# The routing of a per-sample expert convolution: DMA order, column groups of one product, order of the filter bands

## The chip, the cores and the metric

One core of a Trainium2 chip runs the whole program in one launch. The metric is device time in microseconds (us), the median of several runs. "TensorE" or PE is the matrix engine, DVE the vector engine, ACT the scalar engine, POOL is GpSimd, SP the engine whose queue issues the DMAs here (SPq).

## The reference, cut to what matters

The input is 4 images of 64 channels and 128x128 pixels. Four stages follow each other, each `x = x + stage(group_norm(x))`. The change touches the second, a grouped 3x3 convolution whose filters are mixed per image out of four experts:

```
p  = x.reshape(b, c, 16, h//16, 16, w//16).mean(axis=(3, 5))          # pooled to 16x16
r  = relu(einsum('bcij,oc->boij', p, conv_w) + conv_b)                # 16 channels
r  = relu(r.reshape(b, -1) @ fc_w.T + fc_b)                           # 4096 -> 256
rw = sigmoid(r.reshape(b, 4, c))                                      # a gate for each expert and channel
cw = einsum('beo,eoikl->boikl', rw, w_experts)                        # the filters of this image
out = conv3x3(x, cw, feature_group_count=16)
```

The group norm of each stage needs sums over the whole image, so a stage can't start before the one before it has ended. The routing (all lines up to `cw`) needs the whole image too, and the convolution needs `cw`.

## The kernel before, in words

Two images lie side by side on the 128 partitions (64 channels each), and a loop goes twice over such a pair. `X` holds the two images in SBUF. Everything in this text happens between the end of the first stage and the end of the second, once in each pass of that loop.

**Windows.** The convolution works on windows: nine windows of 16 rows, with 8 channels of one image times 16 rows on the partitions. To get there, SP sends `X` to DRAM window by window (L502, `spill`, 1 MB each) and reads each window back in the other layout (`spread`, L489 to L494, into `WN`, in pieces of 512 B). `spread(w)` waits until window `w` has landed in DRAM. The last of them sets `l1_in` to its full count, for which ACT waits (L1879) before it normalizes the first of 16 units (`normed_window`, L1883).

**Order on SP's queue** (L496 to L506). Before the last window's spill SP waits for the last sum of squares of ACT (L499) and sends the four pieces of the routing weights (`FCT`, L501, 1 MB each; `fc_in[0]` counts the first two, `fc_in[1]` the others). Then come the spill of window 8, `spread(7)`, `spread(8)`, and last the table `RT` (L506, 832 KB), which holds the bias `FCB`, the expert filters `EXPW` and the selection matrix `PICK`.

**Product with the weights.** PE (L2172 to L2178) forms the 4096-to-256 product of both images as 32 matmuls, 16 channels `o` times two halves `h` of the 256 pooled pixels. Each has 2 columns of weights (the two images) and streams 256 columns of `FCT`; all accumulate in `PSUM[0:2, 1]`. At `o = 0` PE waits for `fc_in[0]`, at `o = 8` for `fc_in[1]`. A float32 matmul appears in the trace as two passes, so 32 matmuls are 64 records.

**Gates.** DVE waits for the product and for `RT` (L1463, L1464), adds the bias (L1465), takes the maximum with 0 (L1467), ACT takes the exponential (L1878), DVE adds 1 and takes the reciprocal (L1469, L1471). Four small matmuls of PE (L2182) spread the 256 gates over the partitions, into bank 2 of PSUM, in two column groups (output partitions 0 to 63 and 64 to 127).

**Filters and bands.** DVE multiplies `EXPW` with the gates for both images `b` (L1476), and then for each `b` sums over the four experts (L1482, L1485) and writes the values `VAL` (L1488). `toeplitz` (L736 to L752) turns the values of one unit into a banded matrix `WIDE`, by three multiplications (L745) and two additions (L752). DVE makes the bands of units 0 and 1 (`V_UNITS = 2`) after the values of `b = 0` and before those of `b = 1`; POOL makes those of units 2 to 15, after it has waited for all values (`l1_val`, L1689). Units 0 to 7 need the values of `b = 0` only, units 8 to 15 those of `b = 1`.

**Convolution.** PE (L2196 to L2208) takes the 16 units in order, each 9 matmuls of 384 columns (18 records), after `l1_xn` (the unit is normalized) and `l1_tv` or `l1_tp` (its bands are made). ACT evacuates each unit (L1893), DVE adds the residual and takes statistics (L1503 to L1514), SP sends it back to DRAM (L510). For unit 1 ACT waits for all values first (L1889), since its buffer shares memory with the products of `b = 1`.

Of the kernel before, what the change touches and what calls it, by code (L numbers as in the profile page):

```python
# [8 lines left out]
ALU = mybir.AluOpType  # L9
# [4 lines left out]
BATCH, C, H, W = 4, 64, 128, 128  # L14
P = 2 * C
# [13 lines left out]
EXPERTS, RED, FC = 4, 16, 256  # L29
# [51 lines left out]
UNITS = P // WCH  # L81
# [33 lines left out]
def program(nc, x, vec, mat, dts, rows, fc, sel, far_sel, cst, out):  # L115
    ctx = ExitStack()
    with ctx:
# [37 lines left out]
        rt_spill = nc.dram_tensor("rt_spill", (P, NRT), F32).ap()  # L155
# [33 lines left out]
        PSUM = ctx.enter_context(nc.psum_tensor("PSUM", [P, 8, 512], F32))  # L189
# [64 lines left out]
        FS = POOLED  # L254
# [4 lines left out]
        FCT = r.take(RED, 2, FC)  # L259
        RB = r.take(2, 2 * RED)  # L260
        r.at = NREG - TOK - NRT
        RT = r.take(NRT)
        EXPW = RT[:, 0:EXPT]
        FCB = RT[:, EXPT:EXPT + FC]
        PICK = RT[:, EXPT + FC:NRT].rearrange("p (s m) -> p s m", s=2)
# [61 lines left out]
        def steps(*ns):  # L327
# [16 lines left out]
        rt_in, rt_saved = sem("rt_in"), sem("rt_saved")  # L344
        l1_in, l1_xn, l1_sq, l1_pool, l1_mom, l1_bc_pe = steps(
            "l1_in", "l1_xn", "l1_sq", "l1_pool", "l1_mom", "l1_bc_pe")
        l1_val, l1_tv, l1_tp, l1_mm, from_psum, l1_res, l1_st = steps(
            "l1_val", "l1_tv", "l1_tp", "l1_mm", "from_psum", "l1_res", "l1_st")
# [4 lines left out]
        rt_pe, rt_dve, rt_act = sem("rt_pe"), sem("rt_dve"), sem("rt_act")  # L353
# [18 lines left out]
        def settle(eng):  # L372

            eng.sem_inc(settled, 1)
# [89 lines left out]
        def _(sp):  # L464
# [22 lines left out]
            with sp.Fori(0, PAIRS) as pair:  # L487
# [8 lines left out]
                for w in range(WINDOWS):  # L496
                    sp.wait_ge(o_x, pair * NS + (window_strip(w) + 1 + CREDIT))
                    if w == WINDOWS - 1:
                        sp.wait_ge(l1_sq, (pair + 1) * (2 * NS) + CREDIT)  # L499
                        for j in range(4):  # L500
                            sp.dma_start(FCT[:, 4 * j:4 * j + 4], fc[:, 4 * j:4 * j + 4]).then_inc(fc_in[j // 2], 16)  # L501
                    sp.dma_start(spill[w], X[:, STEP * w:STEP * w + WROW, :].rearrange("p r x -> p (r x)")).then_inc(moved[w % 2], 16)  # L502
                    if w >= 1:
                        spread(w - 1)
                spread(WINDOWS - 1)
                sp.dma_start(RT, rt_spill).then_inc(rt_in, 16)  # L506

                for u in range(UNITS):
                    sp.wait_ge(l1_res, pair * UNITS + (u + 1))
# [244 lines left out]
        V_UNITS = 2  # L754
# [348 lines left out]
        def _(dve):  # L1103
# [37 lines left out]
            for s in range(2):  # L1141
                p, q = s * C, s * C + C
# [15 lines left out]
            for s in range(2):  # L1158
                p, q = s * C, s * C + C
                ins = dve.tensor_tensor(W3[p:q, 1, 1, :], W3[p:q, 1, 1, :], NOT3[p:q, p:q], ALU.add)  # L1160
# [7 lines left out]
            for m, half in ((1, 0.5), (2, -0.5)):  # L1168
                ins = dve.scalar_tensor_tensor(out=WCOL[:, :, m, :], in0=W3[:, :, 1, :], scalar=half, in1=W3H,
                                               op0=ALU.mult, op1=ALU.add)  # L1170
# [91 lines left out]
            with dve.Fori(0, PAIRS) as pair:  # L1262
# [193 lines left out]
                q0 = pair * 16  # L1456
# [7 lines left out]
                dve.wait_ge(rt_in, pair * 16 + 16)  # L1464
                dve.tensor_tensor(FS[0:2, :], PSUM[0:2, 1, 0:FC], FCB[0:2, :], ALU.add).then_inc(rt_dve, 1)  # L1465
                dve.wait_ge(rt_dve, q0 + 3)
                dve.tensor_scalar(FS[0:2, :], FS[0:2, :], 0.0, None, ALU.max).then_inc(rt_dve, 1)  # L1467
                dve.wait_ge(rt_act, pair + 1)
                dve.tensor_scalar(FS[0:2, :], FS[0:2, :], 1.0, None, ALU.add).then_inc(rt_dve, 1)  # L1469
                dve.wait_ge(rt_dve, q0 + 5)  # L1470
                dve.reciprocal(FS[0:2, :], FS[0:2, :]).then_inc(rt_dve, 11)  # L1471
                dve.wait_ge(rt_pe, pair * 3 + 3)
                v0 = pair * 16
                n = EXPT // 4
                for b in range(2):
                    dve.tensor_tensor(EPROD[:, b].rearrange("p (a t o) -> p a t o", t=9, o=4),  # L1476
                                      EXPW.rearrange("p (a t o) -> p a t o", t=9, o=4),
                                      PSUM[:, 2, b * P:(b + 1) * P].rearrange("p (a o) -> p a o", o=4).unsqueeze(
                                          2).broadcast_to([P, 32, 9, 4]), ALU.mult).then_inc(l1_val, 1)
                for b in range(2):  # L1480
                    dve.wait_ge(l1_val, v0 + 2 + b if b == 0 else v0 + 6)
                    dve.tensor_tensor(EPROD[:, b, 0:2 * n], EPROD[:, b, 0:2 * n], EPROD[:, b, 2 * n:4 * n],  # L1482
                                      ALU.add).then_inc(l1_val, 1)
                    dve.wait_ge(l1_val, v0 + 4 + 3 * b)
                    dve.tensor_tensor(EPROD[:, b, 0:n], EPROD[:, b, 0:n], EPROD[:, b, n:2 * n], ALU.add).then_inc(l1_val, 1)  # L1485
                    dve.wait_ge(l1_val, v0 + 5 + 3 * b)
                    for h in range(2):
                        ins = dve.tensor_scalar(  # L1488
                            VAL[:, b].rearrange("p k (t c) -> p (k t) c", c=WCH)[:, :, 4 * h:4 * h + 4],
                            EPROD[:, b, 0:n].rearrange("p (a o) -> p a o", o=4), HALF2[:, h:h + 1], None, ALU.mult)  # L1490
                    ins.then_inc(l1_val, 1)
                    if b == 0:
                        dve.wait_ge(l1_val, v0 + 6)
                        for u in range(V_UNITS):
                            toeplitz(dve, l1_tv, pair * 16 + 5 * u, u == 0, u)
                dve.wait_ge(l1_tv, pair * 16 + 5 * V_UNITS)
                dve.sem_inc(l1_tv, 16 - 5 * V_UNITS)
                dve.sem_inc(l1_val, 7)

                for u in range(UNITS):  # L1500
# [151 lines left out]
        def _(pool):  # L1652
            credit(pool, cv_pool, df_w9, df_r1, df_lo, df_add, sc_u)
            pool.memset(PAD[:, :, :], 0.0).then_inc(border, 1)
            with pool.Fori(0, PAIRS) as pair:
# [30 lines left out]

                in_turn(pool, NS // 2, 0, 0, step)

                pool.wait_ge(l1_val, (pair + 1) * 16)  # L1689
                settle(pool)  # L1690
                for u in range(V_UNITS, UNITS):
                    if u >= RING:
                        pool.wait_ge(l1_mm, pair * UNITS + (u - RING + 1))
                        settle(pool)
                    toeplitz(pool, l1_tp, pair * (5 * (UNITS - V_UNITS)) + 5 * (u - V_UNITS), u == V_UNITS, u)
# [50 lines left out]
        def _(act):  # L1746
# [31 lines left out]
            with act.Fori(0, PAIRS) as pair:  # L1778
# [94 lines left out]

                group_norm(pair * 4 + 1)
                act.wait_ge(l1_mom, pair * 16 + 6)
                act.wait_ge(rt_dve, pair * 16 + 4)
                settle(act)
                act.activation(FS[0:2, :], FS[0:2, :], ACT.Exp, scale=-1.0).then_inc(rt_act, 1)  # L1878
                act.wait_ge(l1_in, (pair + 1) * (WINDOWS * 16))  # L1879
# [112 lines left out]
        def _(pe):  # L1992
# [40 lines left out]
            with pe.Fori(0, PAIRS) as pair:  # L2033
# [138 lines left out]
                for o in range(RED):  # L2172
                    if o % 8 == 0:
                        pe.wait_ge(fc_in[o // 8], pair * 32 + 32)
                    for h in range(2):
                        ins = pe.matmul(PSUM[0:2, 1, 0:FC], RB[:, h, :].rearrange("p (s o) -> p o s", s=2)[:, o, :],
                                        FCT[:, o, h, :], start=(o + h == 0), stop=(o == RED - 1 and h == 1))
                ins.then_inc(rt_pe, 1)  # L2178
                pe.wait_ge(rt_dve, pair * 16 + 6)
                for s in range(2):  # L2180
                    for h in range(2):
                        ins = pe.matmul(PSUM[h * C:(h + 1) * C, 2, s * P:(s + 1) * P], PICK[0:2, s, 0:C],  # L2182
                                        FS[0:2, :].rearrange("p (a h o) -> p a h o", h=2, o=4)[:, :, h, :],
                                        start=True, stop=True)
                ins.then_inc(rt_pe, 1)
# [189 lines left out]
```

## Time and profile before

| | |
|---|---|
| time, median of 3 runs | 2608.61 us (2603.66 to 2608.94) |
| span of the profiled execution, first to last instruction | 2604.5 us |
| time of the profiled execution beyond its span | not given on its own; the median of the runs is 4.1 us above that span |
| PE / DVE / ACT / POOL busy | 83% / 74% / 56% / 55% |
| DMA, mean over the span | 60 GB/s |

The span runs from the first to the last instruction. Busy shares are averages over stages of different kinds. Around the change (340 to 481 us for the first pair, 1617 to 1758 us for the second) each stage waits for the one before it, and what counts is the chain of waits in that stretch.

### The profile page before, as it was taken

What the parts mean: (1) busy time and instruction counts of PE and PEld (TensorE: products, weight loads), DVE (VectorE), ACT (ScalarE), POOL (GpSimd) and SP (SyncE); (2) the same over time, 40 slices, a digit from 0 to 9 for tenths busy, and PEclk for the clock granted to TensorE, in tenths of its full rate; (3) what the DMA queues carried; (4) which work ended last, traced back from release to release, by engine and by line L of the source; (5) the groups of instructions that cost most, each with busy time, mean ns of one, the idle gap of its engine ahead of it and who ended that gap; (6) DMA issues with size and microseconds to landing.
All of it is one profiled execution on the core that took longest, in us unless ns stands there. A gap on an engine that the chain in (4) does not pass through costs nothing.

```text
span 2604.5 us, 29243 instructions
## 1 busy us (share of the span) xinstructions
PE 2174.7 (83%) x7607; PEld 1139.6 (44%) x7607; DVE 1932.7 (74%) x3308; ACT 1452.4 (56%) x2268; POOL 1425.8 (55%) x1287
## 2 busy tenths in 40 slices
PE   3898859897968989986988977798789589999788
PEld 2397525443543333332335964353344333333243
DVE  6656746598957999994755668466899399999754
ACT  1743534385865676663346436236678467667532
POOL 2231009378947888872322400475799388888532
PEclk9988879898979999998988989899999799999999
DMA  4000363400000010013820007333000001011145
GB/s 177 1 1 1 136 233 100 175 1 0 1 2 1 17 33 17 17 33 114 242 53 0 1 1 275 130 101 138 1 1 1 3 9 25 17 24 26 51 122 121
DMA packets 131751, 155.97 MB, mean 60 GB/s; under 512 B 4951, under 2 KB 107743, under 8 KB 128247
## 3 DMA queue, kind: packets, MB, share of 16 engines
q1 hardware_dynamic: 131575, 154.00, 19.3%
q8 instruction: 65, 1.06, 0.2%
q14 instruction: 111, 0.91, 0.1%
HBM read 81.69 MB, written 72.29 MB: 59 GB/s over the span
## 4 chain that ended last, share of the span: by engine, by line
PE 39%; DVE 23%; issue 14%; POOL 13%; ACT 5%; DMA 3%; SPq 1%; DVEq 1%; POOLq 0%; ACTq 0%
PE PSUM L2207 7%; PE PSUM L704 7%; POOL BIG L903 6%; PE PSUM L2028 4%; DVE BIG L819 3%; POOL BIG L1733 3%; DVE BIG L843 3%; POOL BIG L1728 3%; PE PSUM L2071 3%; PE PSUM L2085 2%; PE PSUM L2227 2%; DVE PSUM L1086 2%; DVE BIG L850 2%; DVE PSUM L826 2%; DVE BIG L864 2%
## 5 line engine op out<-in xcount | busy, mean ns | idle before, releaser
L903 POOL TENSOR_TENSOR BIG<-BIG 128x512 f32<-128x512 f32 x320 | 406.9, 1272 | 106.1 <-DVE BIG L864 84.3
L819 DVE TENSOR_TENSOR BIG<-PSUM,BIG 128x512 f32<-128x512 f32 x576 | 378.7, 686 | 71.1 <-PE PSUM L1013 28.2
L1086 DVE SCALAR_TENSOR_TENSOR PSUM<-BIG,VECS,PSUM 128x1024 f32<-128x1024 f32 x224 | 288.3, 1287 | 40.3 <-PE PSUM L2028 35.0
L745 POOL TENSOR_TENSOR BIG<-TOEP,BIG 128x384 f32<-128x384 f32 x84 | 97.2, 1183 | 340.5 <-DVE BIG L1488 340.5
L1013 PE MATMUL PSUM<-BIG,SELB 120*128 120x512 bf16 x576 | 211.9, 388 | 81.5 <-DVE BIG L819 73.7
L2028 PE MATMUL PSUM<-BIG,WDW 128*128 128x512 f32 x512 | 233.5, 600 | 11.3 <-ACT BIG L1932 11.3
L2207 PE MATMUL PSUM<-BIG 128*128 128x381 f32 (+1 forms) x576 | 190.4, 494 | 15.2 <-DVE BIG L752 15.2
L1019 PE MATMUL PSUM<-BIG,CSTS 128*128 128x512 f32 x384 | 200.6, 604 | 0.0
L1013 PEld LDWEIGHTS PSUM<-BIG,SELB 120*128 120x128 bf16 x576 | 55.9, 97 | 276.1 <-DVE BIG L819 182.7
L2028 PEld LDWEIGHTS PSUM<-BIG,WDW 128*128 128x128 f32 x512 | 96.7, 192 | 139.2 <-issue 115.5
L1733 POOL TENSOR_TENSOR BIG<-BIG 128x1024 f32<-128x1024 f32 x64 | 150.9, 2357 | 11.7 <-POOL BIG L1728 11.7
L2207 PEld LDWEIGHTS PSUM<-BIG 128*128 128x128 f32 x576 | 111.8, 194 | 93.3 <-issue 20.6
L704 PE MATMUL PSUM<-BIG,WL 128*128 128x512 f32 x256 | 119.5, 610 | 15.5 <-POOL BIG L689 12.3
L955 ACT ACTIVATE BIG<-BIG 128x320 bf16<-128x320 f32 x64 | 30.1, 470 | 168.0 <-POOL BIG L928 168.0
L688 POOL TENSOR_TENSOR BIG<-BIG 128x576 f32<-128x576 f32 x32 | 39.1, 1222 | 153.2 <-issue 96.1
L1706 POOL TENSOR_TENSOR BIG<-BIG 128x1024 f32<-128x1024 f32 x32 | 75.6, 2362 | 77.6 <-ACT BIG L1920 77.6
L1728 POOL TENSOR_SCALAR BIG<-BIG,VECS,CSTS 128x1024 f32<-128x1024 f32 x96 | 114.2, 1196 | 6.8 <-POOL BIG L1733 6.8
L704 PE MATMUL PSUM<-BIG,WMID 128*128 128x512 f32 x256 | 115.5, 594 | 0.3 <-DVE BIG L679 0.2
L1893 ACT ACTIVATE BIG<-PSUM,SMG 128x1152 f32<-128x1152 f32 x32 | 39.0, 1220 | 136.0 <-PE PSUM L2207 113.2
L1019 PEld LDWEIGHTS PSUM<-BIG,CSTS 128*128 128x128 f32 x384 | 75.1, 196 | 74.6 <-issue 69.8
L2260 PE MATMUL PSUM<-BIG,CSTS 128*128 128x512 f32 x128 | 69.8, 672 | 45.3 <-DVE BIG L1086 45.2
L919 POOL TENSOR_TENSOR BIG<-BIG 128x96 f32<-128x96 f32 x192 | 69.1, 389 | 64.8 <-ACT BIG L964 64.8
(362 smaller groups left out, 5387.5 us busy)
## 6 DMA issues: line engine op xcount, KB each, us to landing
spill<-X SPq DMA_DIRECT2D x18, 1024.0 KB, 6.1
back_spill<-BIG SPq DMA_DIRECT2D x32, 576.0 KB, 3.4
X<-x SPq DMA_DIRECT2D x32, 512.0 KB, 7.9
rows_spill<-X SPq DMA_DIRECT2D x64, 256.0 KB, 4.1
out<-BIG SPq DMA_DIRECT2D x64, 256.0 KB, 3.6
BIG<-rows_spill SPq DMA_DIRECT2D x28, 512.0 KB, 5.1
X<-back_spill SPq DMA_DIRECT2D x14, 896.0 KB, 11.6
BIG<-fc SPq DMA_DIRECT2D x8, 1024.0 KB, 9.6
```

Source lines behind the costliest of these rows:

```text
L704: ins = pe.matmul(PSUM[:, 4 * k + m, :].rearrange("p (r j) -> p r j", r=8), w, VC[:, k, m, b:b + 8, :], start=(b == 0), stop=(b == 1))
L745: eng.tensor_tensor(to.rearrange("p (x c r) -> p x c r", x=3, r=WROW), TOEP[:, y].unsqueeze(1).unsqueeze(1).broadcast_to([P, 3, WCH, WROW] ...
L819: dve.tensor_tensor(img(o), img(PSUM[:, (k + q) % 2, :]), pch(c, XBASE, dy, dx), ALU.mult).then_inc(df_p, 1)
L843: dve.tensor_tensor_scan(HH[:, k, :], DA, PSUM[:, BB, :], SM[:, 12:13] if first else HH[:, 1 - k, CH - 1:CH], ALU.mult, ALU.add).then_inc( ...
L903: pool.tensor_tensor(XS[:, k, :], XS[:, k, :], product_buffer(q), ALU.add).then_inc(df_add, 1)
L1013: pe.matmul(PSUM[:, (k + q) % 2, :], SELB[:, q, :], WTB[0:WROWS, k, h * CH:(h + 1) * CH], start=True, stop=True).then_inc(df_w, 1)
L1019: pe.matmul(PSUM[:, ACC, :], ident, PRD[:, m % 2, :], start=(m == 0), stop=(m == PE_SUMS - 1)).then_inc(df_acc, 1)
L1086: return dve.scalar_tensor_tensor(out=rows8(to), in0=strip(c, base, dy, dx), scalar=vc(weights, j), in1=rows8(acc), op0=ALU.mult, op1=ALU.add)
L1728: pool.tensor_scalar(rows8(d_tap if n else d_side[:, c % 2, :]), strip(c, XBASE, dy, dx), vc("dw_w", j), cs("zero")[:, 0:1], ALU.mult, ALU ...
L1733: pool.tensor_tensor(d_side[:, c % 2, :], d_side[:, c % 2, :], d_tap, ALU.add).then_inc(d1_part, 1)
L2028: ins = pe.matmul(img(acc[:, h * CH:(h + 1) * CH]), w[:, j - stored, :], strip(c, base, dy, dx)[:, h * ROWS:(h + 1) * ROWS, :], start=(j = ...
L2207: ins = pe.matmul(to, WIDE[:, u % RING, x, :], v, start=(x == 1), stop=(x == 2))
```

## The change

In the sync block the load of `RT` moves from behind the last `spread` to behind the four loads of `FCT`, which is ahead of the last spill. The product with the weights goes to two column groups: the half `h = 0` accumulates in `PSUM[0:2, 1]`, the half `h = 1` in `PSUM[64:66, 1]`, and DVE adds the second by one more instruction. The gates are spread into bank 6 instead of bank 2. DVE makes products, values and the bands of units 0 and 1 for `b = 0` first, releases POOL by `l1_tv`, and then does all of `b = 1`; POOL waits for the values of `b = 1` only ahead of unit 8. The counts of the semaphores follow.

```diff
                             sp.dma_start(FCT[:, 4 * j:4 * j + 4], fc[:, 4 * j:4 * j + 4]).then_inc(fc_in[j // 2], 16)
+                        sp.dma_start(RT, rt_spill).then_inc(rt_in, 16)
                     sp.dma_start(spill[w], ...).then_inc(moved[w % 2], 16)
                     if w >= 1:
                         spread(w - 1)
                 spread(WINDOWS - 1)
-                sp.dma_start(RT, rt_spill).then_inc(rt_in, 16)
...
                 dve.tensor_tensor(FS[0:2, :], PSUM[0:2, 1, 0:FC], FCB[0:2, :], ALU.add).then_inc(rt_dve, 1)
                 dve.wait_ge(rt_dve, q0 + 3)
+                dve.tensor_tensor(FS[0:2, :], PSUM[C:C + 2, 1, 0:FC], FS[0:2, :], ALU.add).then_inc(rt_dve, 1)
+                dve.wait_ge(rt_dve, q0 + 4)
                 dve.tensor_scalar(FS[0:2, :], FS[0:2, :], 0.0, None, ALU.max).then_inc(rt_dve, 1)
...
                 for b in range(2):
                     dve.tensor_tensor(EPROD[:, b]..., EXPW...,
-                                      PSUM[:, 2, b * P:(b + 1) * P]..., ALU.mult).then_inc(l1_val, 1)
+                                      PSUM[:, 6, b * P:(b + 1) * P]..., ALU.mult).then_inc(l1_val, 1)
-                for b in range(2):
-                    dve.wait_ge(l1_val, v0 + 2 + b if b == 0 else v0 + 6)
+                    dve.wait_ge(l1_val, v0 + 2 + 4 * b)
                     dve.tensor_tensor(EPROD[:, b, 0:2 * n], ...).then_inc(l1_val, 1)
...
                     if b == 0:
-                        dve.wait_ge(l1_val, v0 + 6)
+                        dve.wait_ge(l1_val, v0 + 5)
                         for u in range(V_UNITS):
                             toeplitz(dve, l1_tv, pair * 16 + 5 * u, u == 0, u)
-                dve.wait_ge(l1_tv, pair * 16 + 5 * V_UNITS)
-                dve.sem_inc(l1_tv, 16 - 5 * V_UNITS)
+                        dve.wait_ge(l1_tv, pair * 16 + 5 * V_UNITS)
+                        dve.sem_inc(l1_tv, 16 - 5 * V_UNITS)
                 dve.sem_inc(l1_val, 7)
...
-                pool.wait_ge(l1_val, (pair + 1) * 16)
+                pool.wait_ge(l1_tv, (pair + 1) * 16)
                 settle(pool)
                 for u in range(V_UNITS, UNITS):
+                    if u == UNITS // 2:
+                        pool.wait_ge(l1_val, (pair + 1) * 16)
+                        settle(pool)
...
                     for h in range(2):
-                        ins = pe.matmul(PSUM[0:2, 1, 0:FC], RB[:, h, :]..., FCT[:, o, h, :],
-                                        start=(o + h == 0), stop=(o == RED - 1 and h == 1))
+                        ins = pe.matmul(PSUM[h * C:h * C + 2, 1, 0:FC], RB[:, h, :]..., FCT[:, o, h, :],
+                                        start=(o == 0), stop=(o == RED - 1))
...
-                        ins = pe.matmul(PSUM[h * C:(h + 1) * C, 2, s * P:(s + 1) * P], PICK[0:2, s, 0:C],
+                        ins = pe.matmul(PSUM[h * C:(h + 1) * C, 6, s * P:(s + 1) * P], PICK[0:2, s, 0:C],
```

## Rows read from the trace of the kernel before

**Rows 1.** The page: span, busy time and share of each engine.
```profile
span 2604.5 us, 29243 instructions
PE 2174.7 (83%) x7607; PEld 1139.6 (44%) x7607; DVE 1932.7 (74%) x3308; ACT 1452.4 (56%) x2268; POOL 1425.8 (55%) x1287
```

**Rows 2.** Chain of waits, 330 to 400 us: start, length, what (engine or DMA, line).
```profile
345.23 15.96 DMA spill<-X
362.05 7.73 DMA BIG<-rt_spill
369.87 0.42 DVE BIG L1465
374.12 2.62 DVE BIG L1476 x2
381.68 18.59 PE PSUM L2207 x48
```

**Rows 3.** Timeline, 325 to 400 us: start, length, engine, line, idle before.
```profile
352.44 16.18 PE L2176 MATMUL PSUM<-BIG 128*2 128x256 f32 x64 [4.83 <-DMA BIG<-fc]
352.82 0.13 PEld L2176 LDWEIGHTS PSUM<-BIG 128*2 128x2 f32 x1 [0.30 <-issue]
356.66 0.13 PEld L2176 LDWEIGHTS PSUM<-BIG 128*2 128x2 f32 x1 [0.30 <-issue]
370.32 0.28 DVE L1467 TENSOR_SCALAR BIG<-BIG 2x256 f32<-2x256 f32 x1
371.12 6.29 ACT L1883 ACTIVATE BIG<-BIG,SMG 128x1152 f32<-128x1152 f32 x5
373.42 0.65 PE L2182 MATMUL PSUM<-BIG 2*64 2x128 f32 x8 [4.81 <-DVE BIG L1471]
383.08 1.26 DVE L752 TENSOR_TENSOR BIG<-BIG 128x384 f32<-128x384 f32 x2
384.26 0.75 DVE L1482 TENSOR_TENSOR BIG<-BIG 128x576 f32<-128x576 f32 x1
386.37 2.42 POOL L745 TENSOR_TENSOR BIG<-TOEP,BIG 128x384 f32<-128x384 f32 x3 [171.15 <-DVE BIG L1488]
```

**Rows 4.** Busy time by stretch, with the granted clock (PEclk), DMA share, GB/s.
```profile
352.40:356.80 4.40, 4.36 (x11) 1.38 (x12) 0.00 (x0) 0.00 (x0) 0.00 (x0) 0.50 1.02 354
356.80:361.00 4.20, 4.20 (x21) 1.62 (x19) 0.00 (x0) 0.00 (x0) 0.00 (x0) 0.99 1.00 381
381.60:386.00 4.40, 4.32 (x7) 2.51 (x8) 4.04 (x9) 0.00 (x0) 0.00 (x0) 0.50 0.00 0
```

**Rows 5.** Timeline, 364 to 369 us, PE alone.
```profile
363.70 4.91 PE L2176 MATMUL PSUM<-BIG 128*2 128x256 f32 x22
```

**Rows 6.** DMAs issued at 344.76, 345.23, 361.33 and 362.05: size, us to landing.
```profile
BIG<-fc SPq DMA_DIRECT2D x1, 1024.0 KB, 13.9
spill<-X SPq DMA_DIRECT2D x1, 1024.0 KB, 16.0
BIG<-spill SPq DMA_DIRECT2D x1, 0.5 KB, 6.4
BIG<-rt_spill SPq DMA_DIRECT2D x1, 832.0 KB, 7.7
```

**Rows 7.** Timeline, 1610 to 1690 us, the second pair.
```profile
1629.65 15.87 PE L2176 MATMUL PSUM<-BIG 128*2 128x256 f32 x64 [4.54 <-DMA BIG<-fc]
1647.48 0.41 DVE L1465 TENSOR_TENSOR BIG<-PSUM,BIG 2x256 f32<-2x256 f32 x1 [21.89 <-DMA BIG<-rt_spill]
1659.75 30.69 PE L2207 MATMUL PSUM<-BIG 128*128 128x384 f32 x88 [7.60 <-DVE BIG L752]
```

**Rows 8.** Line L2207, the convolution: what PE waited for, over both pairs.
```profile
  DVE BIG L752: 15.2, 2
```

**Rows 9.** Timeline, 466 to 500 us.
```profile
465.56 11.71 PE L2207 MATMUL PSUM<-BIG 128*128 128x384 f32 x36
466.27 0.99 POOL L752 TENSOR_TENSOR BIG<-BIG 128x384 f32<-128x384 f32 x1 [0.18 <-POOL BIG L752]
```

More of the change, by code:

```diff
@@ L1469, in _ @@
                 dve.tensor_scalar(FS[0:2, :], FS[0:2, :], 1.0, None, ALU.add).then_inc(rt_dve, 1)
-                dve.wait_ge(rt_dve, q0 + 5)
-                dve.reciprocal(FS[0:2, :], FS[0:2, :]).then_inc(rt_dve, 11)
+                dve.wait_ge(rt_dve, q0 + 6)
+                dve.reciprocal(FS[0:2, :], FS[0:2, :]).then_inc(rt_dve, 10)
                 dve.wait_ge(rt_pe, pair * 3 + 3)
@@ L1477, in _ @@
                                       EXPW.rearrange("p (a t o) -> p a t o", t=9, o=4),
-                                      PSUM[:, 2, b * P:(b + 1) * P].rearrange("p (a o) -> p a o", o=4).unsqueeze(
+                                      PSUM[:, 6, b * P:(b + 1) * P].rearrange("p (a o) -> p a o", o=4).unsqueeze(
                                           2).broadcast_to([P, 32, 9, 4]), ALU.mult).then_inc(l1_val, 1)
-                for b in range(2):
-                    dve.wait_ge(l1_val, v0 + 2 + b if b == 0 else v0 + 6)
+                    dve.wait_ge(l1_val, v0 + 2 + 4 * b)
                     dve.tensor_tensor(EPROD[:, b, 0:2 * n], EPROD[:, b, 0:2 * n], EPROD[:, b, 2 * n:4 * n],
                                       ALU.add).then_inc(l1_val, 1)
-                    dve.wait_ge(l1_val, v0 + 4 + 3 * b)
+                    dve.wait_ge(l1_val, v0 + 3 + 4 * b)
                     dve.tensor_tensor(EPROD[:, b, 0:n], EPROD[:, b, 0:n], EPROD[:, b, n:2 * n], ALU.add).then_inc(l1_val, 1)
-                    dve.wait_ge(l1_val, v0 + 5 + 3 * b)
+                    dve.wait_ge(l1_val, v0 + 4 + 4 * b)
                     for h in range(2):
@@ L1875, in _ @@
                 act.wait_ge(l1_mom, pair * 16 + 6)
-                act.wait_ge(rt_dve, pair * 16 + 4)
+                act.wait_ge(rt_dve, pair * 16 + 5)
                 settle(act)
@@ L2175, in _ @@
                     for h in range(2):
-                        ins = pe.matmul(PSUM[0:2, 1, 0:FC], RB[:, h, :].rearrange("p (s o) -> p o s", s=2)[:, o, :],
-                                        FCT[:, o, h, :], start=(o + h == 0), stop=(o == RED - 1 and h == 1))
+                        ins = pe.matmul(PSUM[h * C:h * C + 2, 1, 0:FC], RB[:, h, :].rearrange("p (s o) -> p o s", s=2)[:, o, :],
+                                        FCT[:, o, h, :], start=(o == 0), stop=(o == RED - 1))
                 ins.then_inc(rt_pe, 1)
-                pe.wait_ge(rt_dve, pair * 16 + 6)
+                pe.wait_ge(rt_dve, pair * 16 + 16)
                 for s in range(2):
                     for h in range(2):
-                        ins = pe.matmul(PSUM[h * C:(h + 1) * C, 2, s * P:(s + 1) * P], PICK[0:2, s, 0:C],
+                        ins = pe.matmul(PSUM[h * C:(h + 1) * C, 6, s * P:(s + 1) * P], PICK[0:2, s, 0:C],
                                         FS[0:2, :].rearrange("p (a h o) -> p a h o", h=2, o=4)[:, :, h, :],
```

## The prediction

> **What bounds the kernel now.** The page gives PE 83% and DVE 74% of the span [rows 1], an average over stages with different limits, so the place of the change has to be read by itself. I read four views, in this order. The chain of waits between the first stage's end and the first matmul of the convolution is the main one [rows 2]: it holds almost no PE work. From 345.23 to 361.2 it is the last spill on its way to DRAM, then the table `RT` behind the last spread, which lands at 362.05 + 7.7 = 369.8 [rows 2, 6], and from 369.87 to 381.68 a string of short DVE, ACT and PE steps up to the first convolution matmul. The reader is to see that the table ends the wait of L1465, with the product close behind it: PE's 64 passes run from 352.44 to 352.44 + 16.18 = 368.6 [rows 3], 1.2 us before the table. Second, the timeline of the convolution: once started PE waits for nobody; the only wait of L2207 on an engine is the first one of each pair, 15.2 us in 2 times, for the bands of unit 0 [rows 8]. So whatever brings the first matmul of L2207 forward brings the end of the stage forward by as much, and every later stage, since each needs sums over the whole image. Third, the landing times [rows 6], since a DMA moved ahead of others delays them. Fourth, the stretches with the granted clock [rows 4].
>
> **The change part by part**, worked out for the first pair; the second is the same shape, with its own start times.
>
> *The table sent ahead.* It stands on SP's queue behind the four weight loads and ahead of spill 8, spread 7 and spread 8. The last weight load lands at 344.76 + 13.9 = 358.7, spill 8 at 345.23 + 16.0 = 361.2, 2.5 us later for 1 MB [rows 6]. At that rate 832 KB take 2.0 us, so the table lands near 360.7, and spill 8, both spreads and `l1_in` come 2.0 us later. `l1_in` lies at 361.33 + 6.4 = 367.7 now [rows 6], at 369.8 then. What does that hold up? ACT's normalization of unit 0, at 6.29 / 5 = 1.26 us a unit (I take 1.4) [rows 3]: unit 0 is ready at about 369.8 + 0.2 + 1.4 = 371.4. That is a floor for PE, used below. The bounds: nothing at all if the rings have room, and 7.7 us, the whole time of the table in its own row. I take 2.0, the rate of the neighbouring transfer. The issue itself is 2 us or less on SP, and SP then only waits for a spill that is on the rings until 361: hidden.
>
> *Two column groups.* Now each pass starts when the one before it has streamed. At the low clock (0.50, 1.2 GHz) ten loads stand from 352.82 to 356.66, 3.84 / 9 = 0.427 us apart; at the full clock (2.4 GHz) 22 passes take 4.91 us, of which the last is 0.38, so (4.91 - 0.38) / 21 = 0.216 us apart [rows 3 to 5]. Do passes to two column groups run at once? No row shows this product so, but one shows such a pair of groups: L2182, 8 passes of 128 columns in 0.65 us [rows 3]. One pass of 256 columns takes 0.216, so one of 128 takes 0.108; eight in turn would take 0.86 us and the end of the last one on top. They took 0.65, which fits four slots of 0.108 and an end of 0.2. So two passes share a slot. I apply that: 32 slots instead of 64. The low clock lasts until 356.8 [rows 4], that is 10 slots (20 passes); the 12 left of the first half of the weights take 6 x 0.216 = 1.3, to 358.1. There PE now meets a wait that it did not have before: the second half lands at 358.7. Then 16 slots x 0.216 = 3.5 and an end of 0.16: the product is complete at 362.4, 6.2 us earlier, and the table is there (360.7). Bounds: from this to no overlap at all, 368.6.
>
> A rule that speaks against this part: the Trainium skill, "TensorE: Matmul & The Clock Gate", section "Packing small matmuls — row/col tiling", says that a weight load overlaps running matmuls only where the row groups differ, and here both groups use all rows. The trace disagrees for loads under matmuls of the same rows: L2176's loads stand inside a PE stretch without a gap [rows 3]. The same section measured 2.38x for three column groups; by that share two groups would give 1.59x and a slot of 0.27 us, which makes the product end 1.2 us later than my sum.
>
> *The added addition.* One DVE instruction of 2x256 reading PSUM; the one like it is the first L1465, from 369.87 to the start of L1467 at 370.32 [rows 2, 3]: +0.45 us on the path. Bounds: 0.28, the cheaper form of the same size, and 0.45.
>
> *`b = 0` first.* Of the two L1476 (2.62 us together [rows 2]) one leaves the path: -1.31, and a wait for its own result comes in, for which the neighbours show about 0.1: -1.2. The steps of `b = 1` (1.3 for its product, 0.75 for L1482 [rows 3], and the rest until POOL's start at 386.4) now lie behind the second band. Nothing needs them before ACT's second evacuation and DVE's first residual, more than 9 us after PE's start: hidden. If that cover failed it would cost up to 1.3 + 386.4 - 384.3 = 3.4 us.
>
> *POOL released earlier.* POOL starts now at 386.37 [rows 3] and finishes unit 15 at 466.27 + 0.99 = 467.3 [rows 9]. PE needs it 4 us after that (its work ends at 465.56 + 11.71 = 477.3 [rows 9], and a unit takes 5.8, half of that row). So POOL isn't the bound before. After the change it starts when DVE's second band is done, 383.08 + 1.26 - 381.68 = 2.7 us after PE's start instead of 4.7 [rows 2, 3]: its margin grows by 2 us. POOL and DVE are then busy together for 3 us, where they were not; even at 1.1 us more for the first unit the margin stays. Worth: nothing. Bank 6 instead of 2 costs nothing: it only lets PE write unit 0 while DVE still reads the gates.
>
> *Sum.* From the start of L1465 to the first L2207 it is 381.68 - 369.87 = 11.81 now, and 11.81 + 0.45 - 1.2 = 11.06 then. L1465 starts at 362.45, so L2207 at 373.5, above the floor of 371.4. Gain 8.2 us. Second pair [rows 7]: product from 1629.65; its clock rises after about 3.9 us, so 9 slots low and 7 high give 1635.0; the second half of the weights, lying as in the first pair, lands near 1636.1, product ends 1639.7; the chain is 1659.75 - 1647.48 + 0.45 - 1.2 = 11.5; L2207 at 1651.3, gain 8.5. Together 16.7 us. In either pair PE begins the convolution at the low clock, as it does now (0.50 from 381.6 to 386 [rows 4]), since it idles 6 us ahead of it; where the rise falls may shift it by 1 us each way. Against the profiled execution: span 2604.5 - 16.7 = 2587.8; what lies around that span is not given, and the median of the runs is 4.1 above it, so I put the time at 2608.6 - 16.7 = 2591.9.
>
> **The rivals.**
>
> *No overlap.* The passes to two groups run one after the other. For it: no row has two groups with 128 rows and a long stream. Against it: L2182's 0.65 us. The product then ends at 368.6 and 1645.5, the table no longer ends the wait, and L1465 starts 1.2 and 1.9 us earlier; with 0.75 of the shorter chain each the gain is 2.0 + 2.7 = 4.7: 2603.9 us.
>
> *The windows become the bound.* The table pushes `l1_in` so far that unit 0's normalization is later than its bands. My margin is 373.5 - 371.4 = 2.1 us; it decides when the table costs the rings more than 4.1 us. For it: its own 7.7 us from issue to landing [rows 6], and the rings are full from 352 to 361 (share 1.0) [rows 4]. Against it: it is smaller than a transfer that took 2.5. At 7.7, unit 0 is ready at 377.1, the gain is 4.6 a pair: 2599.4 us.
>
> *Slower: loads exposed.* If, with column groups, a load had to wait until the pass of the other group is through, each of the 64 passes would take its whole 0.38 plus its load, 0.46 at the full clock and more at the low one: about 32 us for the product, an end near 385 and a loss of 15 - 0.8 = 14 us a pair: 2637 us. It turns the sign when the product takes over 352.44 to 370.6, 18.2 us, or 0.28 us a pass; L2182 had a pass every 0.08 to 0.11 at half the columns.
>
> That the change doesn't do what it says is the first rival for the product; for the DMA it can't be, the order on the queue is the program's.
>
> **How the numbers follow.** Forecast 0.75, no overlap 0.12, windows as the bound 0.09, slower 0.03, 0.01 for others. The forecast's own range is 2588 to 2596 (partial overlap adds 2.4 us in two pairs, the clock's rise 2, and the runs of before are 5 us apart). The range reaches to the windows' case: 2586 to 2600, and leaves out the 0.15 of no overlap and slower. 0.2% (5.2 us) is about what a measurement of this kernel can tell from no change. Faster by more than that: forecast and windows' case, 0.84. Within it: no overlap, 0.12. Slower: 0.04.
>
> **What the changed kernel's profile would show.** L2176: 64 passes in some 10 us, with a short wait for the second half of the weights; starts in pairs. L1465 ended by PE, not by the table, at about 362.4. `l1_in`'s last spread landing 2 us later than now. L1883 starting before L2207 and not ending its wait. L2207's first matmul at about 373.5 and 16 units without a gap behind it; POOL starting about 376. If L2176 takes 16 us again, the overlap was wrong; if L2207's first wait ends on ACT L1883, the cost of the table on the rings was; if L2207 waits for POOL or ACT in the middle, the cover of `b = 1` was.

## The result, and the profile after

The changed kernel takes 2593.27 us (median of 6 runs, 2591.36 to 2598.74) against 2608.36 us (6 runs): 0.9938 of the time before, 95% interval 0.9922 to 0.9954, some 16 us faster. The span of its profiled execution is 2589.1 us, 15.4 below the 2604.5 of [rows 1].

The chain of waits of the first pair is the place to look. Columns: start, length, what.

```profile
344.38 8.53 DMA BIG<-fc
352.95 8.85 PE PSUM L2180 x64
361.83 0.42 DVE BIG L1465
362.27 0.43 DVE BIG L1467
366.54 1.36 DVE BIG L1478
372.96 27.27 PE PSUM L2211 x78
```

Two links are gone: the last spill's 15.96 us and the table's 7.73 us of [rows 2] stand in the chain no more. In their place are the weights' transfer and the product itself (line 2180 now, 2176 before). The timeline has the rest; its columns are start, length, engine, line, and the idle time before with what ended it:

```profile
352.95 8.82 PE L2180 MATMUL PSUM<-BIG 128*2 128x256 f32 x64 [5.62 <-DMA BIG<-fc]
353.34 0.13 PEld L2180 LDWEIGHTS PSUM<-BIG 128*2 128x2 f32 x2 [0.29 <-issue]
353.76 0.13 PEld L2180 LDWEIGHTS PSUM<-BIG 128*2 128x2 f32 x2 [0.29 <-issue]
361.83 0.41 DVE L1465 TENSOR_TENSOR BIG<-PSUM,BIG 2x256 f32<-2x256 f32 x1 [14.00 <-PE PSUM L2180]
370.70 6.30 ACT L1887 ACTIVATE BIG<-BIG,SMG 128x1152 f32<-128x1152 f32 x5 [7.08 <-DMA BIG<-spill]
372.96 22.46 PE L2211 MATMUL PSUM<-BIG 128*128 128x384 f32 x63 [6.47 <-DVE BIG L752]
375.86 2.94 POOL L745 TENSOR_TENSOR BIG<-TOEP,BIG 128x384 f32<-128x384 f32 x3 [159.28 <-DVEq L1498]
```

The same 64 passes take 8.82 us where they took 16.18 [rows 3]; the loads come two at a time, still 0.42 us apart at the low clock. The first addition is released by PE, no longer by the table, and the first convolution matmul comes at 372.96 instead of 381.68 [rows 2]. In the second pair the trace names another releaser:

```profile
1639.31 2.25 PE L2211 MATMUL PSUM<-BIG 128*128 128x384 f32 x3 [6.47 <-ACT BIG L1887]
```

The prediction took a wait that ends on ACT's normalization (L1887 now, L1883 before) as the sign that the table had cost the rings too much. Here it isn't. In the first pair PE starts before ACT is done with its second unit, so it needs the first alone, and that one was ready at 1638.05. The bands of unit 0 (L752) were done at 1639.16, 0.15 us before PE's start, as in the first pair; it is ACT's second unit that happens to end at 1639.29.

All runs below are measured by one number, the **stretch** from the issue of the first load of the group (L501) to the first convolution matmul. It was 381.68 - 341.78 = 39.9 us in the first pair and 1659.75 - 1619.29 = 40.5 in the second. It is now 372.96 - 341.51 = 31.5 and 1639.31 - 1608.61 = 30.7. That is 18.2 us in both pairs, while the span fell by 15.4. The rest was given away where nothing was changed: from the second pair's first convolution matmul to the end of the span it took 2604.5 - 1659.75 = 944.8 us before and 2589.1 - 1639.31 = 949.8 now. The largest piece stands in the second pair's third stage, in the same instructions, before (first fence) and after (second). Columns: stretch, its length, busy us of PE, PEld, DVE, ACT, POOL, then the granted clock:

```profile
2025.00:2035.00 10.00, 5.49 (x26) 3.45 (x24) 1.48 (x2) 7.01 (x9) 0.00 (x0) 0.84 0.00 0
```

```profile
2005.00:2018.00 13.00, 8.49 (x24) 5.19 (x23) 1.48 (x2) 6.47 (x8) 0.00 (x0) 0.50 0.00 0
```

Two dozen matmuls take 8.5 us at 1.2 GHz where they took 5.5 at mostly 2.4 GHz. All three profiled executions of the changed kernel have this piece: the 16 small matmuls in it take 3.43 us in each, against 1.85 before. But it doesn't hang on the change alone, as the kernels b_together, ballast and best2 below have it fast (1.87 to 2.00). The part from the second pair's convolution to the end takes 948.0 to 953.7 us in all runs below. Why the clock falls here in one kernel and there in another stays open; it is why the stretch says more of an edit than one execution's span.

### The profile page after: what moved, and what is told of

Its sections match the earlier page's. It is cut to its first block, busy times and chain, and to the rows that moved or that the text cites. A ratio compares the mean times of both kernels' runs of the same rounds, so it can differ in the third digit from the quotient of the medians.

```text
span 2589.1 us, 29247 instructions
## 1 busy us (share of the span) xinstructions
PE 2157.4 (83%) x7607; PEld 1133.4 (44%) x7607; DVE 1937.9 (75%) x3310; ACT 1453.2 (56%) x2268; POOL 1427.5 (55%) x1287
## 4 chain that ended last, share of the span: by engine, by line
PE 39%; DVE 22%; issue 15%; POOL 13%; ACT 6%; DMA 3%; SPq 1%; DVEq 1%; POOLq 0%; ACTq 0%
PE PSUM L2211 7%; POOL BIG L903 6%; PE PSUM L704 6%; PE PSUM L2032 4%; DVE BIG L819 3%; POOL BIG L1732 3%; POOL BIG L1737 3%; DVE BIG L843 3%; PE PSUM L2075 3%; PE PSUM L2089 2%; PE PSUM L2231 2%; DVE PSUM L1086 2%; DVE BIG L850 2%; DVE PSUM L826 2%; PE PSUM L2047 2%
## 5 line engine op out<-in xcount | busy, mean ns | idle before, releaser
L819 DVE TENSOR_TENSOR BIG<-PSUM,BIG 128x512 f32<-128x512 f32 x576 | 379.0, 687 | 73.3 <-PE PSUM L1013 30.2
L1086 DVE SCALAR_TENSOR_TENSOR PSUM<-BIG,VECS,PSUM 128x1024 f32<-128x1024 f32 x224 | 288.3, 1287 | 38.2 <-PE PSUM L2032 32.5
L2211 PEld LDWEIGHTS PSUM<-BIG 128*128 128x128 f32 x576 | 111.2, 194 | 90.2 <-ACT BIG L1887 13.4
L704 PE MATMUL PSUM<-BIG,WL 128*128 128x512 f32 x256 | 120.1, 613 | 15.4 <-POOL BIG L689 12.3
L955 ACT ACTIVATE BIG<-BIG 128x320 bf16<-128x320 f32 x64 | 30.1, 470 | 167.4 <-POOL BIG L928 167.4
## 6 DMA issues: line engine op xcount, KB each, us to landing
X<-back_spill SPq DMA_DIRECT2D x14, 896.0 KB, 11.6
```

Of the source, the lines that this page charges most:

```text
L704: ins = pe.matmul(PSUM[:, 4 * k + m, :].rearrange("p (r j) -> p r j", r=8), w, VC[:, k, m, b:b + 8, :], start=(b == 0), stop=(b == 1))
L819: dve.tensor_tensor(img(o), img(PSUM[:, (k + q) % 2, :]), pch(c, XBASE, dy, dx), ALU.mult).then_inc(df_p, 1)
L1086: return dve.scalar_tensor_tensor(out=rows8(to), in0=strip(c, base, dy, dx), scalar=vc(weights, j), in1=rows8(acc), op0=ALU.mult, op1=ALU.add)
L2211: ins = pe.matmul(to, WIDE[:, u % RING, x, :], v, start=(x == 1), stop=(x == 2))
```

## The experiments

Four rounds of comparison gave these numbers; "ratio" is to the kernel before in the same rounds. The stretch is from one profiled execution each, first and second pair.

| kernel | stretch, us | median, us | ratio, 95% interval |
|---|---|---|---|
| before | 39.9 / 40.5 | 2608.4 to 2613.2 | 1 |
| after | 31.5 / 30.7 | 2593.3 | 0.9938 (0.9922 to 0.9954) |
| again | 31.0 / 31.5 | 2592.2 | 0.9928 (0.9915 to 0.9942) |
| again_b | 31.0 / 32.0 | 2594.0 | 0.9934 (0.9918 to 0.9950) |
| no_groups | 37.4 / 37.8 | 2602.9 | 0.9968 (0.9956 to 0.9980) |
| table_last | 40.2 / 39.8 | 2612.2 | 1.0003 (0.9993 to 1.0014) |
| b_together | 33.2 / 32.5 | 2594.6 | 0.9923 (0.9908 to 0.9938) |
| best | 31.3 / 31.2 | 2589.0 | 0.9912 (0.9898 to 0.9925) |
| best2 | 30.1 / 30.2 | 2590.5 | 0.9914 (0.9897 to 0.9931) |
| best2_b | 31.3 / 30.2 | 2591.8 | 0.9928 (0.9911 to 0.9944) |
| ballast | 33.5 / 33.1 | 2594.9, one run | |
| four_groups | 31.6 / 31.5 | 2594.2, one run | |
| groups_32 | 31.5 / 31.4 | 2590.8, one run | |
| pool_late | 30.7 / 31.2 | 2589.5, one run | |

Times and stretches agree only to some 3 to 5 us. By its ratio no_groups gains 8.4 us and b_together 20.1; by their stretches, 5.2 and 14.7. The stretch carries the argument below, and the times support it only where the difference is larger than that.

**Theory A**: the two column groups run at once, the table's early load makes that visible, and PE starts the convolution earlier by the sum of both. **Theory B**: one of the two carries the gain alone.

**again** and **again_b**, no edit: the changed kernel beside the others.

> The changed kernel once more, in the same rounds as the next three, as their measure. From the issue of the first weight load to the first convolution matmul it took 31.5 and 30.7 us in the profiled execution after (39.9 and 40.5 before). Expected: the same within 1 us, and 2593 us, 15 less than before. Both theories below expect this.

> The changed kernel once more, as the measure for 'best2_b' in the same rounds: 2592 to 2594 us, stretch from the first weight load to the first convolution matmul 30.7 to 31.5 us.

As expected, except that the second pair of again_b took 32.0 us. Over its six stretches the changed kernel has a mean of 31.3 us with a spread of 1.3. Part of the spread is the clock of the gates' matmuls (L2182 before): they took 0.65 us in four of the six and 1.11 to 1.12 in the second pairs of again and again_b, as in the second pair of the kernel before (1.11).

**no_groups.** One part undone:

```diff
-ins = pe.matmul(PSUM[h * C:h * C + 2, 1, 0:FC], ..., start=(o == 0), stop=(o == RED - 1))
+ins = pe.matmul(PSUM[0:2, 1, 0:FC], ..., start=(o + h == 0), stop=(o == RED - 1 and h == 1))
-dve.tensor_tensor(FS[0:2, :], PSUM[C:C + 2, 1, 0:FC], FS[0:2, :], ALU.add).then_inc(rt_dve, 1)
```

> The changed kernel with the product in one column group again (and without the second addition). Theory A (the two groups run at once, and that is most of the gain): 64 passes take 16 us again, so the product ends near 369 and the first convolution matmul comes at 361.8 -> 369.1, less 0.45 for the addition, 38.3 us after the first weight load; time near 2604, 4 to 5 below before. Theory B (the gain comes from the table being sent ahead, the product's length being hidden by the transfer): the stretch stays near 31 to 33 us and the time near 2594.

Its timeline:

```profile
350.14 16.18 PE L2178 MATMUL PSUM<-BIG 128*2 128x256 f32 x64 [4.58 <-DMA BIG<-fc]
366.36 0.41 DVE L1465 TENSOR_TENSOR BIG<-PSUM,BIG 2x256 f32<-2x256 f32 x1 [20.30 <-PE PSUM L2178]
```

The product is back at 16.18 us (16.04 in the second pair, 15.87 before), and DVE waits for it, while the table had landed 7.6 and 7.1 us before the product's end. 6.3 us of the gain of 8.9 a pair are gone. Theory A holds for the product.

**table_last.** The table's load back behind the last spread:

```diff
-                        sp.dma_start(RT, rt_spill).then_inc(rt_in, 16)
...
                 spread(WINDOWS - 1)
+                sp.dma_start(RT, rt_spill).then_inc(rt_in, 16)
```

> The changed kernel with the table's load back behind the last spread. Theory A: the product still ends near 359 to 362, but the first addition waits for the table, which lands at 369.8, so the stretch is 39.2 us (11.1 us of chain behind it) and the time near 2607: the two parts give their gain only together. Theory B': the column groups carry the gain alone; the stretch is near 32 us. ACT's first normalization should come 2 to 3 us earlier than in the changed kernel (368 instead of 370.7).

```profile
368.48 0.41 DVE L1465 TENSOR_TENSOR BIG<-PSUM,BIG 2x256 f32<-2x256 f32 x1 [22.29 <-DMA BIG<-rt_spill]
370.18 5.04 ACT L1887 ACTIVATE BIG<-BIG,SMG 128x1152 f32<-128x1152 f32 x4
372.48 1.12 PE L2186 MATMUL PSUM<-BIG 2*64 2x128 f32 x8 [11.51 <-DVE BIG L1473]
```

DVE waits for the table again, as in [rows 7], and the whole gain is gone, though the product is fast. Theory B falls on both sides: the groups without the early table give nothing (1.0003), the early table without the groups 0.9968. It is 0.6 to 1.0 us worse than I had expected in the stretch: PE idles 11.5 us ahead of the gates' matmuls and does them at the low clock, 1.12 us for 0.65, and in the first pair the table landed 0.5 us later than before (28.5 us after the first load). The 1.2 us that the order of `b` saves doesn't show either, since the added addition (0.45) and, in the first pair, that low clock (0.47) stand against it. ACT's early normalization did not show; ACT was held behind the exponential, which waits for the same table.

**b_together.** DVE's order of before, and POOL's wait for all values:

```diff
+for b in range(2):
+    dve.tensor_tensor(EPROD[:, b]..., ALU.mult)          # both products first
 for b in range(2):
-    dve.tensor_tensor(EPROD[:, b]..., ALU.mult)
...
-pool.wait_ge(l1_tv, (pair + 1) * 16)
+pool.wait_ge(l1_val, (pair + 1) * 16)
```

> The changed kernel with DVE's order of before: both products (L1476 twice) ahead of the values and bands of the first half, and POOL released only when all values are made. Theory A: only the second product's 1.3 us, less 0.1, comes back on the path: the stretch from the first weight load to the first convolution matmul is 1.2 us longer, 32.2 to 32.7 us, and PE waits for nobody after it, since POOL's unit 2 is ready some 5 us before PE needs it; 2595 us, 2.4 more than the changed kernel, hardly to be told by its time. Rival: POOL's earlier release is worth something of its own; PE would then show waits for POOL in the convolution.

From the first addition to the convolution it is 375.01 - 362.73 = 12.3 and 12.7 us against 11.1 and 11.6 in "again": 1.15 a pair, the term of the sum. The first pair's stretch of 33.2 lies above the range expected, as its last weights landed 13.6 us after their issue and its product ended 20.8 us after the first load, later than in any of the changed kernel's six stretches (19.5 to 20.4). The time can't tell it from the changed kernel. PE waited for POOL nowhere.

**pool_late.** Only POOL's release undone, DVE's order kept:

```diff
 pool.wait_ge(l1_tv, (pair + 1) * 16)
 settle(pool)
+pool.wait_ge(l1_val, (pair + 1) * 16)
+settle(pool)
```

> The changed kernel, but POOL waits for the values of both images again before its first band; DVE's order stays. Theory A: POOL starts 3 us later (about 6 us after PE's first convolution matmul instead of 2.9), DVE's steps of the second image run at 0.75, 0.46 and 0.65 us (they took 0.95, 0.97 and 1.27 beside POOL), PE still waits for nobody after its first matmul, and the stretch and the time are those of the changed kernel. Rival: POOL's early start is part of the gain; then PE waits for bands and the time is some us higher.

```profile
371.23 17.14 PE L2213 MATMUL PSUM<-BIG 128*128 128x384 f32 x46 [6.47 <-DVE BIG L752]
375.44 0.76 DVE L1483 TENSOR_TENSOR BIG<-BIG 128x576 f32<-128x576 f32 x1
376.23 0.46 DVE L1486 TENSOR_TENSOR BIG<-BIG 128x288 f32<-128x288 f32 x1
377.55 2.43 POOL L745 TENSOR_TENSOR BIG<-TOEP,BIG 128x384 f32<-128x384 f32 x3 [162.04 <-DVE BIG L1489]
```

Against the changed kernel, where POOL runs beside these steps:

```profile
377.16 0.95 DVE L1483 TENSOR_TENSOR BIG<-BIG 128x576 f32<-128x576 f32 x1
378.15 0.97 DVE L1486 TENSOR_TENSOR BIG<-BIG 128x288 f32<-128x288 f32 x1
```

The early release is worth nothing: PE's first wait is its only one here too, and the stretch is the same. The release costs DVE 0.2 and 0.5 us on two steps that nobody waits for.

**ballast.** Two more transfers of the table's size ahead of the last spill:

```diff
 sp.dma_start(RT, rt_spill).then_inc(rt_in, 16)
+for j in range(2):
+    sp.dma_start(ballast[j], rt_spill).then_inc(load, 16)    # DRAM to DRAM
```

> The changed kernel with two more transfers as large as the table (832 KB each, DRAM to DRAM, read by nobody) behind the table and ahead of the last spill. Theory A: the product and the gates don't notice (first addition 20.0 to 20.5 us after the first weight load), while the last spread lands 4 to 5 us later: ACT's first normalization starts near 33 us after the first weight load, not 27.6 to 29.2, and ends the wait of the first convolution matmul at 34.5 to 35 us, not 31.0 to 31.5. This is the case 'windows become the bound', forced. Rival: the chain sets the start still, at 31.5, if ballast costs the rings under 2 us in all; or the table itself lands later, if what follows it matters as theory C says.

```profile
359.72 0.41 DVE L1469 TENSOR_TENSOR BIG<-PSUM,BIG 2x256 f32<-2x256 f32 x1 [13.73 <-PE PSUM L2184]
371.79 3.83 ACT L1891 ACTIVATE BIG<-BIG,SMG 128x1152 f32<-128x1152 f32 x3 [10.27 <-DMA BIG<-spill]
373.19 2.28 PE L2215 MATMUL PSUM<-BIG 128*128 128x384 f32 x3 [8.67 <-ACT BIG L1891]
```

The rival "windows become the bound", made real: the first addition keeps its place (20.0 and 19.7 us after the first load), ACT's normalization starts at 32.1 and 31.7 us, and now it ends PE's wait, 1.4 us later. The stretch grew by 2 us, less than the 3.5 expected, as the ballast delayed the windows by about 4 us on a slack of 2. In the six stretches of the changed kernel unit 0 is normalized 0.9 to 2.8 us before PE starts, 1.8 in the mean: so far away is its next bound.

**four_groups** and **groups_32**, on the array:

```diff
+g = 32 * (2 * (o % 2) + h)                                  # four_groups
-ins = pe.matmul(PSUM[h * C:h * C + 2, 1, 0:FC], ...)
+ins = pe.matmul(PSUM[g:g + 2, 1, 0:FC], ...)
+ins = pe.matmul(PSUM[h * 32:h * 32 + 2, 1, 0:FC], ...)      # groups_32
```

> The changed kernel with the product in four column groups (output partitions 0, 32, 64, 96: parity of o times h), and three additions behind it. If four passes run at once: 64 passes in 16 slots, in the first half four starts per slot of 0.427 us; the product waits for the second half of the weights and ends 8 slots (1.7 us) + 0.2 after its landing, near 16.4 + 1.9 = 18.3 us after the first weight load, but the table lands at 20.1 and the two further additions cost 0.9, so the first convolution matmul comes 0.5 to 0.9 us later than in the changed kernel. If only two run at once: two starts per slot, the product ends as in the changed kernel.

```profile
352.04 3.59 PE L2185 MATMUL PSUM<-BIG 128*2 128x256 f32 x32 [4.83 <-DMA BIG<-fc]
357.00 3.26 PE L2185 MATMUL PSUM<-BIG 128*2 128x256 f32 x32 [1.37 <-DMA BIG<-fc]
360.46 0.41 DVE L1465 TENSOR_TENSOR BIG<-PSUM,BIG 2x256 f32<-2x256 f32 x1 [12.75 <-DMA BIG<-rt_spill]
```

```profile
352.00:355.60 3.60, 3.56 (x32) 0.99 (x32) 0.00 (x0) 0.00 (x0) 0.00 (x0) 0.50 1.00 417
357.00:360.30 3.30, 3.26 (x32) 1.00 (x32) 0.00 (x0) 0.00 (x0) 0.00 (x0) 0.58 0.93 384
```

Four passes do run at once: 32 passes in 8 slots of 0.427 and an end. Yet the second half took 3.3 us, not the 1.9 I expected, since the granted clock was low through most of it (0.58). The table (360.4) then held DVE back anyway, and two further additions ate what was left.

> The changed kernel with the second half of the product at output partitions 32 and 33 instead of 64 and 65. Theory A (a group is 32 columns wide for weights of 2 columns, so that neighbours run at once): two starts in every slot as before, product and stretch as in the changed kernel (8.8 to 9.4 us and 30.7 to 31.5). Rival (the array is split in halves of 64): 64 passes in turn, 16 us, stretch 38.

The product took 9.1 and 9.5 us, the stretch 31.5 and 31.4: neighbouring groups of 32 columns do as well as 64 apart, for weights of 2 columns.

**best, best2, best2_b.** A version meant to beat both, and its variant with the filters ahead of the spill:

```diff
+sp.dma_start(RT[0:2, EXPT:NRT], rt_spill[0:2, EXPT:NRT]).then_inc(rt_in, 16)     # 4 KB, first
 for j in range(4):
-    sp.dma_start(FCT...).then_inc(fc_in[j // 2], 16)
+    sp.dma_start(FCT...).then_inc(fc_in[j], 16)
-sp.dma_start(RT, rt_spill).then_inc(rt_in, 16)
+sp.dma_start(EXPW, rt_spill[:, 0:EXPT])...    # best: behind the last spill; best2: here
...
-dve.tensor_scalar(FS, FS, 0.0, None, ALU.max); dve.tensor_scalar(FS, FS, 1.0, None, ALU.add)
+dve.tensor_scalar(FS, FS, 1.0, 1.0, ALU.min, ALU.add)       # after the exponential
```

> Changed kernel with the loads cut to what each step needs: only the two partitions of bias and selection go ahead of the weights, the expert filters go behind the last spill, each quarter of the weights has a semaphore of its own, and the maximum with 0 becomes a minimum with 1 of the exponential, in the instruction that adds 1. Theory A: the product starts 2.5 us earlier and ends 0.2 + 8 slots of 0.216 us behind the last quarter of the weights (about 359.9 instead of 361.8), the chain is 0.45 shorter, and the windows become the bound: the last spread lands near 370, the first convolution matmul comes 1.4 us later, at 371.3 to 371.5 instead of 373.0. The stretch is 30 us (from 31.5), the time 2590 to 2592, not to be told from the changed kernel by its time. A rival: the expert filters behind the spill land too late (after 364.5) and the chain waits for them: stretch 31 or more.

> As 'best', but the expert filters (576 KB) stand behind the weights and ahead of the last spill. In 'best' the last quarter of the weights landed 13.9 us after its issue, with the spill right behind it; in the changed kernel, with the table behind it, 12.6. Theory C (a load lands later when a spill to DRAM stands right behind it on the queue): here it lands after 12.6 again, the product ends near 359.9, the chain gives 371.0 and the windows, 371.4, become the bound: stretch 29.5 to 30.2 us against 31.0 to 31.5. Rival: the landing depends on the rings' total only; it stays at 13.9 and the stretch at 31.

> The kernel 'best2' once more, beside the changed kernel on the same chip. Its stretch was 30.1 and 30.2 us, 2.1 us shorter in both pairs together than the changed kernel's 31.5 + 30.7 (or 31.0 + 31.5). Theory A expects 2 us less in the time, 0.08%: its median 1 to 3 us below that of 'again_b', the intervals overlapping. Rival: the finer waits and split loads cost something elsewhere, and it is not below.

"best" has no shorter stretch than the changed kernel: its last quarter of the weights landed 14.0 and 14.3 us after its issue instead of 12.5 to 13.1, so the earlier start of the product ended in waits of 0.8 and 2.0 us. The chain from the first addition to the convolution shrank by 0.16 us (10.97 for 11.13, first pair), not by the 0.45 expected, and it stayed the bound: PE's wait ends on DVE's bands and not on ACT, in all pairs of best, best2 and best2_b. Its time is lower (2589.0 against 2592.2 in the same rounds, each of its five runs below each of the five of "again"), and I can show no cause for that.

"best2" was to cure the late weights by my theory C and didn't: with a load behind it the last quarter landed after 14.1 and 13.4 us (14.2 and 14.0 in best2_b). In no_groups, where the table stands behind it as in the changed kernel, it landed after 14.3 us in one pair and 12.6 in the other. Theory C falls. Three of the four stretches of best2 are 30.1 to 30.2, 1.1 us below the mean of the changed kernel, one is 31.3. In the only rounds that had both, its median is 2.2 us below that of "again_b", 0.1%, with intervals that overlap. So best2 has the shortest stretches and best the lowest time, and the runs don't prove either better than the changed kernel.

## Why the prediction was right

The forecast was 16.7 us from two earlier starts of the convolution; the six stretches of the changed kernel give 2 x (40.2 - 31.3) = 17.8, the times about 16, 17 and 19 (ratios times 2608 to 2611). That the one forecast time, 2591.9, lies 1.4 us from the measured 2593.3 is in part luck, as the unchanged rest of the kernel moves by more than that from run to run.

The forecast's landing times against those of the six stretches of the changed kernel, in us after the issue of the first weight load, first and second pair of the kernel before:

| | before | forecast | changed kernel (mean) |
|---|---|---|---|
| last of the weights lands | 16.9 / 16.8 | 16.9 | 15.6 to 16.7 (16.0) |
| product complete | 26.8 / 26.2 | 20.6 / 20.4 | 19.5 to 20.4 (20.0) |
| table lands | 28.0 / 28.1 | 18.9 | 18.5 to 20.2 (19.1) |
| last spread lands | 26.0 / 25.9 | 28.0 | 27.5 to 29.1 (28.0) |
| first convolution matmul | 39.9 / 40.5 | 31.7 / 32.0 | 30.7 to 32.0 (31.3) |

- **What bounds it** held: after its first matmul PE waited for nobody in any kernel, and the convolution then took 94.2 to 95.7 us in all of them, so what comes off the stretch comes off the stage, to within 1.5 us.
- **Column groups.** Shown by no_groups and by the double loads. The price of a slot was right; the 0.65 us of L2182 [rows 3] was enough to find it. The estimate from the Trainium skill, "TensorE: Matmul & The Clock Gate", section "Packing small matmuls — row/col tiling", a share of 2.38x for three groups, would have given 1.59x; here 64 passes with the low clock at their start took 8.82 instead of 16.18 us, 1.83x, and four groups ran four to a slot at the low clock. The loads weren't exposed, though both groups use all rows. The product ended some 0.6 us earlier than forecast, because the last weights landed 0.8 us earlier in the mean than in the kernel before, whose landing time I had carried over. That term was off, and it makes the gain 17.8 us instead of 16.7.
- **The table on the rings.** I took 2.0 us for it. In the mean of the six stretches the last spread landed 2.1 us later than before, so the term was right, but the single values lie between 1.5 and 3.1. The profiled execution of the result has the largest: the weights' last quarter landed at 345.32 + 12.6 = 357.9 and the table at 346.05 + 15.6 = 361.65, 0.1 us before the product's end:

```profile
BIG<-rt_spill SPq DMA_DIRECT2D x1, 832.0 KB, 15.6
spill<-X SPq DMA_DIRECT2D x1, 1024.0 KB, 17.7
```

  There the rival "the windows become the bound" was only 0.9 us away (unit 0 ready at 372.05 against 372.96), where I had 2.1 of margin. It happened in none of the six.
- **Added addition**: 362.27 - 361.83 = 0.44 for 0.45. **`b = 0` first**: 1.15 in b_together for 1.2. **Chain**: 11.1 us in four of the six stretches and 11.6 in the two where the gates' matmuls ran at the low clock, for a forecast of 11.06 in the first pair and 11.5 in the second.
- **POOL's release**: worth nothing, shown by pool_late. Its margin was no part of the gain.
- **"No overlap"** was priced at 4.7 us; no_groups, which is that case without the added addition (0.45 a pair, so 5.6 by the same sum), gained 5.2 by its stretches.
- **What I didn't see** is that the two larger parts give their gain only together. I had added up one path, which was right, but with the table last the change is worth nothing, and I had no rival for that.

## What to carry to other kernels

Where several things end close together (here product at 368.6, table at 369.8, windows at 367.7) no single edit shows its worth: price the path after all of them, and ask of each alone what stands right behind it. A matmul with few columns of weights (here 2) and a long stream can be cut over column groups at the cost of one short addition for each further group. What is needed first should be sent first, but only as far as the next bound allows: a table ahead of the windows is paid by the windows.

## What the runs showed of the hardware

Passes to different column groups start in the same slot, with 128 rows, 2 columns of weights and 256 columns streamed: two of them at 1.2 GHz (0.427 us a slot) and at 2.4 GHz (0.216), four of them at 1.2 GHz.

The transfers' rate falls to two thirds for some 2 us near where the loads give way to the spill, and what is in flight then lands late: here the table, in the kernel before and in the first pair of no_groups the last of the weights. The first fence has before, the second after; the last column is GB/s.

```profile
351.00:354.00 3.00, 1.56 (x4) 0.47 (x5) 0.00 (x0) 0.00 (x0) 0.00 (x0) 0.50 1.01 418
354.00:356.00 2.00, 2.00 (x6) 0.65 (x5) 0.00 (x0) 0.00 (x0) 0.00 (x0) 0.50 0.98 274
```

```profile
353.00:356.00 3.00, 3.00 (x16) 0.95 (x18) 0.00 (x0) 0.00 (x0) 0.00 (x0) 0.50 0.99 415
356.00:358.00 2.00, 2.00 (x20) 0.75 (x18) 0.00 (x0) 0.00 (x0) 0.00 (x0) 0.87 1.09 281
```

With ballast between them the table landed 343.65 + 14.4 - (343.18 + 12.8) = 2.1 us behind the weights instead of 3.7 (2.0 to 3.8 in the six stretches of the changed kernel). The fall isn't bound to come: in the second pair of b_together, with the same order on the queue, the rate stayed at 414 to 423 GB/s from 1627 to 1633 us, and the table landed 2.0 us behind the weights. Which of the transfers is hit, and why, stays open.

DVE's additions of 576 and 288 elements took 0.95 and 0.97 us beside a busy POOL, 0.76 and 0.46 without it. In four_groups 64 passes in two stretches of 3.6 and 3.3 us, 1.4 us apart, stayed near 1.2 GHz (0.50, 0.58), where in the changed kernel one unbroken product rose to 2.4 GHz after 3.7 us.
